# Attention stores its accumulators undivided; inverse sums travel through DRAM and the division moves to the mixing stage

## The reference

```python
qkv = x @ c_attn_w.T + c_attn_b                 # 16 heads of 16
q_lat, k_lat, v_lat = q @ q2l_w.T + q2l_b, k @ kv2l_w.T + kv2l_b, v @ kv2l_w.T + kv2l_b   # latents of 32
q_lat, k_lat = rope(q_lat), rope(k_lat)
att = einsum('bhql,bhkl->bhqk', q_lat @ wqk_w.T + wqk_b, k_lat) * 32 ** -0.5
att = softmax(where(causal, att, -inf))
y = (einsum('bhqk,bhkl->bhql', att, v_lat) @ l2o_w.T + l2o_b).transpose(0, 2, 1, 3).reshape(B, T, C)
x = layernorm(x + y @ cproj_w.T + cproj_b)
logits = relu(x @ rw1 + rb1) @ rw2 + rb2        # router over 8 experts, the best 2 of each token
x = layernorm(x + weighted sum of the two experts' outputs, 1024 places per expert)
```

## Time and profile before

| | us |
|---|---|
| timed runs, median of 3 | 2879.03 |
| profiled execution: span, first to last instruction | 2899.6 |
| TensorE matmul busy in it | 2746.4 (95%) |
| VectorE busy | 2128.1 (73%) |
| ScalarE busy | 1811.4 (62%) |
| GpSimd busy | 802.8 (28%) |

### The profile page before, as it was taken

How to read it: one execution, slowest core, us unless ns; L and a number is a source line. 1 busy time by engine, 2 the same in 40 slices (tenths; PEclk the granted TensorE clock), 3 DMA queues, 4 the chain that set the end, 5 groups by cost and what they waited for, 6 DMA issues and landing times. The chain is left out here.

```text
span 2899.6 us, 47875 instructions
## 1 busy us (share of the span) xinstructions
PE 2746.4 (95%) x16538; PEld 1913.0 (66%) x16538; DVE 2128.1 (73%) x5590; ACT 1811.4 (62%) x3353; POOL 802.8 (28%) x785
## 2 busy tenths in 40 slices
PE   8999989999999999999999999999799995999991
PEld 7888755666666666666566666665377773999991
DVE  7888889988898888888888888887144543545444
ACT  5666626667667766777776677776554452555554
POOL 7888720110111111111011111101125444133322
PEclk9999979999999999999999999999899997999996
DMA  7788853432522424343252343330333211334326
GB/s 227 271 276 282 283 134 72 96 84 56 123 72 73 109 73 98 81 117 78 56 123 59 73 93 83 76 78 7 103 127 107 95 65 47 92 84 108 73 25 239
DMA packets 259522, 320.28 MB, mean 110 GB/s; under 512 B 70562, under 2 KB 157643, under 8 KB 258000
## 3 DMA queue, kind: packets, MB, share of 16 engines
q1 hardware_dynamic: 241616, 294.02, 36.0%
q0 software_dynamic: 17664, 23.19, 4.0%
HBM read 182.69 MB, written 143.95 MB: 113 GB/s over the span
## 5 line engine op out<-in xcount | busy, mean ns | idle before, releaser
L1027 ACT ACTIVATE att_probs<-att_score_bank 128x512 f32<-128x512 f32 (+1 forms) x2240 | 1131.7, 594 | 462.7 <-PE att_score_bank L954 449.6
L1082 DVE TENSOR_REDUCE att_partial_max<-att_max_bank 128x1 f32<-128x512 f32 x1536 | 983.1, 684 | 163.1 <-PE att_max_bank L940 162.5
L954 PE MATMUL att_score_bank<-att_q_st,att_k_st 98*128 98x512 f32 (+3 forms) x1792 | 574.4, 382 | 6.4 <-DMA att_q_st<-att_max_rows 4.6
L940 PE MATMUL att_max_bank<-att_k_st,att_q_st 96*128 96x512 f32 (+3 forms) x1792 | 566.3, 372 | 0.8 <-DVE att_partial_max L1086 0.2
L1067 POOL TENSOR_SCALAR_AFFINE_SELECT att_probs<-att_probs 128x512 f32<-128x512 f32 x256 | 162.6, 637 | 1406.0 <-ACT att_probs L1027 1406.0
L971 PE MATMUL att_acc_bank<-att_probs,att_v_st 128*32 128x512 f32 (+3 forms) x5120 | 528.5, 535 | 0.2
L1086 DVE CUSTOM_DVE_ANT_0 att_edge_sum<-att_max_bank,first_edge 128x256 f32<-128x256 f32 (+3 forms) x1024 | 460.8, 485 | 57.6 <-PE att_max_bank L940 56.9
L954 PEld LDWEIGHTS att_score_bank<-att_q_st,att_k_st 98*128 98x128 f32 x1792 | 319.1, 190 | 172.5 <-ACT att_probs L1027 83.2
L940 PEld LDWEIGHTS att_max_bank<-att_k_st,att_q_st 96*128 96x128 f32 x1792 | 330.7, 190 | 122.9 <-DVE att_partial_max L1082 49.9
L971 PEld LDWEIGHTS att_acc_bank<-att_probs,att_v_st 128*32 128x32 f32 x5120 | 136.5, 109 | 245.9 <-issue 133.5
L242 POOL TENSOR_TENSOR proj_op_low<-proj_turned,proj_op_high 128x512 fp32r<-128x512 f32 x192 | 244.6, 1300 | 47.1 <-ACT proj_op_high L402 45.1
(11 more groups left out here) (239 smaller groups left out, 4451.8 us busy)
## 6 DMA issues: line engine op xcount, KB each, us to landing
qk_parts<-proj_parts SPq DMA_DIRECT2D x64, 1024.0 KB, 5.2
att_k_st<-qk_parts SPq DMA_DIRECT2D x168, 256.0 KB, 6.1
att_q_st<-qk_parts SPq DMA_DIRECT2D x159, 256.0 KB, 4.2
v_tokens<-proj_v_tok SPq DMA_DIRECT2D x64, 256.0 KB, 4.6
att_v_st<-v_tokens SPq DMA_DIRECT2D x64, 256.0 KB, 6.8
exp_w<-in_ew SPq DMA_DIRECT2D x16, 1024.0 KB, 8.1
first_q<-qk_parts SPq DMA_DIRECT2D x33, 256.0 KB, 4.2
dispatched<-att_empty_rows SPq DMA_DIRECT2D x8, 1036.0 KB, 4.1
```

Of the source, the lines that this page charges most:

```text
L940: last = nc.tensor.matmul(max_ps[u % MAXB][:, at:end], q_tile(n)[0:3 * L, head, tile * P:(tile + 1) * P], k_tile(g, kb)[0:3 * L, head, 0:e ...
L954: last = nc.tensor.matmul(score_ps[h % SCOREB][:, i * (CH - q0):(i + 1) * (CH - q0)], k_tile(g, kt // TT)[:, j + i, (kt % TT) * P:(kt % TT ...
L1027: nc.scalar.activation(probs[:, k % PROBS, j:j + heads, q0:CH], score_ps[h % SCOREB][:, 0:heads * (CH - q0)].rearrange("p (j n) -> p j n", ...
L1082: nc.vector.tensor_reduce(partial_max[:, m % 2, j * TT + t, kb:kb + 1], bank[:], AX.X, ALU.max).then_inc(unit_reduced, 1)
```

## The change

In attention, `turn_sums`, `divide` and `bias_y` go, with their tiles and semaphores, and with the turns in `Order`. ScalarE's copy of the accumulator is stored as it is, 32 rows per head by 512 queries, undivided. SP loads the sums alone in the form of 128 x 64 for 512 tokens, VectorE inverts these, SP stores the inverses to DRAM, waits for that, and loads them with each head's row repeated on 16 partitions. The values come in already turned; `scale_y` on VectorE multiplies them with the spread inverses into `yt`. `turn_y` and `copy_y` go. The inverses of the first two chunks and the spread of the first are made in the last two slots of attention. The bias of the values is folded into `kept.b_out`, group by group. In `experts` two semaphores become one.

```diff
+def load_values(sp, d, chunk, yk, done):
+    for k in range(KC):
+        sp.dma_start(yk[:, k],
+                     heads_of(d)[chunk, k * P // HD:(k + 1) * P // HD, 0:HD]).then_inc(done, 16)
+def load_sums(sp, d, chunk, sums, done):
+    sp.dma_start(sums,
+                 heads_of(d)[chunk, :, HD].rearrange("h (i n) -> h i n", n=PARTS_OF_SUMS)).then_inc(done, 16)
+def store_recips(sp, d, chunk, recips, done):
+    sp.dma_start(d["recip"][chunk].rearrange("h (i n) -> (h i) n", n=PARTS_OF_SUMS), recips).then_inc(done, 16)
+def load_recips(sp, d, chunk, rk, done):
+    for k in range(KC):
+        src = d["recip"][chunk, k * P // HD:(k + 1) * P // HD]
+        sp.dma_start(rk[:, k],
+                     src.unsqueeze(1).broadcast_to([P // HD, HD, CH])).then_inc(done, 16)
...
-            nc.vector.tensor_scalar(bias_col[:], ones[:], lat[0][0][0:64, 64:65], l2o_b[:], ALU.mult, ALU.add).then_inc(weights_done, 1)
+            for g in range(G):
+                last = nc.vector.tensor_scalar(bias_col[:, g], ones[:], lat[0][0][0:64, 64 + g:65 + g], l2o_b[:],
+                                               ALU.mult, ALU.add)
+            last.then_inc(weights_done, 1)
...
             def store_y(n):
-                sp.wait_ge(y_biased, n + 1)
-                sp.dma_start(d["y"][b, c, :, :, col:col + HG * HD],
-                             y[:, n % 2].rearrange("p t j e -> p t (j e)")).then_inc(y_out[n % 2], 16)
+                sp.wait_ge(acc_read, n + 1)
+                sp.dma_start(d["y"][g // G, c, g % G], y_raw[:, n % 2]).then_inc(y_out[n % 2], 16)
...
                 if kt == 0 and n:
-                    pe.wait_ge(y_done, n)
+                    pe.wait_ge(acc_read, n)
...
             def read_acc(n):
                 act.wait_ge(weighted, LAST_STEP[n])
                 if n >= 2:
-                    act.wait_ge(y_done, n - 1)
+                    act.wait_ge(y_out[n % 2], 16 * (n // 2))
...
+            def sums_of(chunk):
+                load_sums(sp, d, chunk, sums[:, chunk % SUBS], sums_in[chunk % SUBS])
+            def spread(chunk):
+                buf = chunk % SUBS
+                sp.wait_ge(recip_done, chunk + 1)
+                store_recips(sp, d, chunk, recips[:, buf], recips_out)
+                sp.wait_ge(recips_out, 16 * (chunk + 1))
+                sp.wait_ge(y_scaled, KC * (chunk - SUBS + 1))
+                load_recips(sp, d, chunk, rk[buf], recip_in[buf])
...
             def step(c):        # SP
-                    load(chunk[3], (c[1] + 3) % SUBS)
+                    load(chunk[3])
+                if not is_last(c, 2):
+                    spread(c[1] + 2)
+                if not is_last(c, 4):
+                    sums_of(c[1] + 4)
...
             def step(c):        # TensorE
-                if not is_last(c, 2):
-                    turn_y(after(c, 2))
                 second_layer(c)
...
+            def scale_y(c):
+                buf = c[1] % SUBS
+                ready(dve, chunk_in[buf], count(c, 48, 48, bufs=SUBS))
+                ready(dve, recip_in[buf], count(c, 16 * KC, 16 * KC, bufs=SUBS))
+                ready(dve, mixed, count(c, 2))
+                for k in range(KC):
+                    nc.vector.tensor_tensor(yt[:, k], yk[buf][:, k], rk[buf][:, k], ALU.mult).then_inc(y_scaled, 1)
...
             def step(c):        # VectorE
                 split_x1(c)
+                if not is_last(c, 2):
+                    recips_of(after(c, 2))
                 if not is_first(c):
                     n = choose(after(c, -1))
                 if not is_last(c, 1):
                     moments_of(after(c, 1))
                 if not is_first(c):
                     place(after(c, -1), n)
+                if not is_last(c, 2):
+                    scale_y(after(c, 2))
```

More of the change, by code:

```diff
@@ L377, in _ @@
             for g in range(G):
-                last = nc.tensor.matmul(lat[1][0][:, 0:C], bias_col[:], cproj[:, g], start=(g == 0), stop=(g == G - 1))
+                last = nc.tensor.matmul(lat[1][0][:, 0:C], bias_col[:, g], cproj[:, g], start=(g == 0), stop=(g == G - 1))
             last.then_inc(folded, 1)
@@ L600 @@
 class Plan:
-    __slots__ = ("now", "last", "tiled", "u", "h", "w", "t", "vector", "scalar", "pool", "reduced", "exped", "ready",
-                 "weighed", "rows", "read", "divided", "before", "kind", "due")
+    __slots__ = ("now", "last", "tiled", "u", "h", "w", "vector", "scalar", "pool", "reduced", "exped", "ready",
+                 "weighed", "rows", "read", "before", "kind", "due")
     def copy(self):
         p = Plan()
[L608 to L611, removed]
+        (p.now, p.last, p.tiled, p.u, p.h, p.w, p.vector, p.scalar, p.pool, p.reduced, p.exped, p.ready, p.weighed,
+         p.rows, p.read) = (
+            self.now, self.last, self.tiled, self.u, self.h, self.w, self.vector, self.scalar, self.pool,
+            self.reduced, self.exped, self.ready, self.weighed, self.rows, self.read)
         p.before = self
@@ L687, in weigh @@
         if KS[k][2] == 0 and n:
-            if plan.divided[0] < n - 1:
-                return None
-            free = max(free, plan.divided[1])
+            free = max(free, plan.read)
         start = max(plan.now + INTO_TILES * (not plan.tiled),
@@ L698, in weigh @@
             p.read = p.scalar + 0.05
[L699 to L706, removed]
         return p
@@ L724, in search @@
         p.now = p.last = p.vector = p.scalar = p.pool = 0.0
-        p.tiled, p.u, p.h, p.w, p.t = False, 0, 0, 0, 0
+        p.tiled, p.u, p.h, p.w = False, 0, 0, 0
         p.reduced, p.exped, p.weighed = (0.0,) * MAXB, (0.0,) * SCOREB, (0.0,) * PROBS
-        p.ready, p.rows, p.read, p.divided = (), (), None, (-1, 0.0)
+        p.ready, p.rows, p.read = (), (), 0.0
         p.before = p.kind = None
         plans = [p]
-        for _ in range(NU + NS + NK + CHUNKS):
+        for _ in range(NU + NS + NK):
             alike = {}
@@ L1129, in _ @@
                     combine_max(UNITS_THROUGH.index(u + 1))
[L1130 to L1134 removed]
+                if u + 1 == UNITS_THROUGH[chunk_of(SLOTS - 1, 0)]:
+                    first_recips()
 EPS = 1e-5
@@ L1465, in norm @@
                                          scale=rstd[:, sub, t:t + 1]).then_inc(x1_done, 1)
-            def copy_y(c):
-                for k in range(KC):
-                    ready(act, y_turned, count(c, KC, k + 1))
-                    if not is_first(c):
-                        ready(act, mixed, count(c, 2))
-                    nc.scalar.activation(yt[:, k], xt_ps[k][:], ACT.Copy).then_inc(turned_copied, 1)
             def step(c):
@@ L1510, in split_x1, with recips_of @@
                                             ALU.subtract).then_inc(x1t_split, 1)
+            def scale_y(c):
[3 more added lines that the diff above has]
+                ready(dve, mixed, count(c, 2))
+                for k in range(KC):
+                    nc.vector.tensor_tensor(yt[:, k], yk[buf][:, k], rk[buf][:, k], ALU.mult).then_inc(y_scaled, 1)
+            def recips_of(c):
+                buf = c[1] % SUBS
+                ready(dve, sums_in[buf], count(c, 16, 16, bufs=SUBS))
+                nc.vector.reciprocal(recips[:, buf], sums[:, buf]).then_inc(recip_done, 1)
             def moments_of(c):
```

210 lines of the change are left out of this document (86 added, 124 removed).

## The result

The changed kernel takes 2891.7 us (median of 4 runs, 2890.2 to 2896.7), the kernel before 2881.1 beside it: a ratio of 1.0043, 95% interval 1.0031 to 1.0055. The two medians differ by 10.6 us; 2842 was forecast.

What follows compares the result with a forecast made beforehand. It took TensorE to bound attention and mixing, with VectorE close behind in attention. Terms 28.2 + 6 + 1.8 + 0.4 + 0.7 = 37 us off the median 2879.03 gave 2842 us, range 2816 to 2862.

Steps and rivals of the forecast that it cites:

- the slack of the round trip in mixing: Mixing steps: reciprocals go to DRAM and return spread, scaled values ready 5.4 us before TensorE wants them; cost 0.
- Rival 3: Mixing: the reciprocals' round trip is late in every step, 2.9 us each, 41 lost; 2883 us, chance 0.05.
- the same 37 off the median: Whole kernel: the 37 us gain reckoned on the profiled span of 2899.6 was taken off the timed median, 2879.03.
- VectorE's term (6): Attention: of 43.2 us of VectorE work removed, TensorE feels 6 us, bounds 8 lost to 15 gained.
- TensorE's 28.2: Attention: four transposes per chunk go, 0.44 us for each of 64 chunks, gained in full, 28.2 us.
- Rival 2: Attention: the planner's new order wastes part of the gain, leaving 17 to 20 us; 2861 us, chance 0.13.
- Rival 1: Attention: VectorE sets the pace, so its 43.2 us are gained, 46 in all; 2833 us, chance 0.16.
- The transposes of mixing: Mixing steps: TensorE's 8 transposes per step cover a wait for ScalarE, so removing them gives only 0.7 us.
- Multiplies and reciprocal hidden: Mixing steps: VectorE's added multiplies (1.4 us) and reciprocal (0.3 us) fall in its idle time; cost 0.
- Edge of the stages and start: From attention's last copy into mixing: 1.8 us gained at the edge, 0.4 us at mixing's start.
- Projection and experts 0: Projection's three more column fills and experts' two semaphores made one: 0 us.
- Wider loads at half the rate: Mixing: by the skill's rule, 256 KB loads use 8 engines, half the rate; values then ready about 2262.4, still ahead of TensorE.

Runs made afterwards that it cites:

- e1: The kernel before, unchanged, profiled once more in a single run: span 2879.5 us.
- e8: The kernel before without VectorE's reciprocal and multiply and GpSimd's bias add per chunk in attention, TensorE's transposes kept: 7.9 us faster.
- e7: The kernel before without TensorE's four transposes of each chunk's accumulator in attention, their places left empty in the order: 6.5 us faster.
- e12: The kernel before, its order unchanged, without attention's transposes, reciprocal, multiply and bias add, accumulator free with ScalarE's copy: 12 us faster.
- e13: Kernel of e9 with the planner of the kernel before, each turn's place left empty: 14.6 us slower than e9.
- e4: The changed kernel with TensorE's four transposes per chunk put back in attention, 63 of 64, unread: 31 us more.
- e9: Changed kernel, mixing steps with reciprocals made a step earlier and their store and spread both issued ahead of SyncE's loads: 2858 us.
- e11: The changed kernel without store and spread of the reciprocals in the mixing steps; what stays of sums, reciprocals and multiplies costs 1 us at most.
- e14: The changed kernel with one edit, reciprocals' store and spread ahead of the loads in SyncE's mixing step: 2856.9 us, ratio 0.9915 to the kernel before.
- e5: Changed kernel, mixing steps with the reciprocals' store ahead of SyncE's loads and reciprocals made a step earlier: no better than with the store moved alone.
- e6: The kernel before with an unused 128x64 VectorE reciprocal added ahead of the choice of experts in 14 mixing steps: 2.3 us less.

## Why the prediction was wrong

- **The step that failed: the slack of the round trip in mixing.** The prediction gave it 5.4 us and a cost of 0. In the late step shown above it was overdrawn by 2.9. Four terms were off, and they add up. The queue was seen rightly, the store behind the loads, but it leaves 9.96 us after the step's mixing begins, not 8.3 (1.6 lost; three loads take 1.8 us to issue, not 1.2, and start later). Behind 1 MB of loads it takes 5.76 us (5.7 to 6.5 in 12 of the 14 steps), not the 2.2 of a store on an idle queue (3.6 lost). The spread takes 5.57 us up to the multiplies, not 3.9 (1.7 lost; 5.0 to 5.7 in the steps in time, 5.6 to 6.4 in the late ones, where the 512 KB store of the normalized rows is issued 1.9 to 2.3 us behind it). And TensorE comes back after 19.7 us, not 21.23 (1.5 lost). 5.4 - 8.4 = -3.0, the 2.9 seen. Even with steps of 21.23 the values would have been 1.5 us late.
- **Rival 3 named the mechanism**, with a chance of 0.05. Its price of 2.9 us per step is close to the measured 2.7 (37.5 / 14) by luck: it had the worst landing of both transfers in every step, where in fact seven of 14 steps waited 2.7 to 4.0 us and paid some 1.7 more for the clock.
- **The base was one execution 20 us above the timed runs**, and the prediction took that offset as evenly spread ("the same 37 off the median"). Most of it sat in mixing, in the step length on which the slack rests. The rows had a sign of it: TensorE busy for 309.5 us of 335 in a stage said to be led by it. In that execution TensorE waited 13.6 us, in 14 waits, for ScalarE's hidden activations, of which e1 has none, and an instruction of the choice of experts stood beside GpSimd's add, 1.8 to 3.1 us long, in 8 of 14 steps, in e1 in none. Which of these is the cause, and what began it, is open.
- **A late value costs more than the wait.** The prediction counted only the wait; behind each of the seven waits the matmuls ran at a granted clock of 0.67 or so, some 1.7 us more.
- **Attention: right in direction, 24.3 us instead of 34** (19 to 24 by the other profiles with the same attention). VectorE's term (6) came out as sized, 5.2 in attention and 7.9 in the time (e8), though only in the old order. TensorE's 28.2 was the term that was mis-sized. It took 99% busy for "no idle time to hide it", while the weight loads' waits of 104.7 and 81.8 us stood in the earlier trace rows. In the order written with turns only 6 of it come out (e7), and those waits grow by 27.9. Both parts together give 8.6 (e12), and the order written anew 15.8 (e13). Rival 2 had the right place, the new order, and the wrong sign; that its number for attention, 20, is near the measured one is luck. Rival 1 fell in the old order: with all of VectorE's 43 us gone attention is 5.2 shorter (e8). In the new order no run puts VectorE's work back, but 63 turns of TensorE cost 30 us there in full (e4), which speaks against VectorE setting the pace. That a turn without cover costs 0.48 us shows that the price itself was read well from the earlier trace rows.
- **The transposes of mixing were free**: right. Steps are 19.7 us with them (e1) and without (e9), and the 0.78 us wait has taken their place.
- **Multiplies and reciprocal hidden**: right (e11). **Edge of the stages and start**: 2.2 predicted, 1.5 measured. **Projection and experts 0**: right, from the first mixing matmul of the last chunk to the end 502.8 us in e1 and in the changed kernel.
- **Wider loads at half the rate**, the rule of the Trainium skill (DMA: Bandwidth & Descriptors, the section on why a DMA increments its semaphore by 16) on the slowest dimension: the trace agrees. The last spread of the changed kernel has the queue to itself. Its 512 KB, in two loads with a slowest dimension of 8, move from 2371.82 to 2375.18 at 156 GB/s with the DMA engines busy for 0.50 of the time; the store of the normalized rows, also 512 KB, moves from 2385.6 in 1.67 us at 311 GB/s and 0.88. Those 1.7 us more are about as much as the spread's term was short. They don't decide the matter alone: ahead of the loads, the same spread costs nothing (e9, e14).

## What to carry to other kernels

Before a slack is reckoned from a profile, its execution's span has to be held against the timed runs; where it is off, find the stage that holds the difference, or count the slack with the shortest step that the engine's own work allows. A transfer's landing time has to be taken for its place in the queue: here the same 32 KB store landed in 1.5 us ahead of 1 MB of loads and in 5.7 to 6.5 behind them, so the short transfer that someone waits for goes ahead of the long ones that nobody does. What an operation costs in an order written by a planner is known only together with the order that is written without it.

## What was not expected of the hardware

VectorE's small instructions are held up beside a GpSimd add of two SBUF operands. In e5:

```profile
2188.13 0.19 DVE L1568 TENSOR_TENSOR mix_cand<-mix_rest,mix_top 128x32 f32<-128x32 f32 x1
2188.36 3.08 DVE L1569 TENSOR_TENSOR mix_cand<-mix_cand,mix_rev 128x32 f32<-128x32 f32 x1
2191.47 0.19 DVE L1570 TENSOR_REDUCE mix_rank<-mix_cand 128x4 f32<-128x32 f32 x1
```
```profile
2188.95 2.42 POOL L1347 TENSOR_TENSOR mix_xb<-kept_xr,kept_b_out 128x1024 f32<-128x1024 f32 x1
```

The multiply of 0.19 us takes 3.08 and ends with the add, at 2191.4. It starts 0.6 us before the add does, so either the add's recorded start is late or it holds VectorE earlier than the trace shows. The Trainium skill (SBUF — State Buffer, the section on the two separate sides) says that a VectorE operation with two SBUF inputs and a GpSimd operation that reads SBUF take a shared port pair in turn, each for its whole length, the first to start going first. The trace agrees in that VectorE stands for the add's 2.4 us and more; by the recorded starts VectorE was first here, and it was held up all the same. It cost nothing where it caught the last instruction of the choice (10 steps of e6, 3 of e14, all of 19.7 us). Whether it costs something in the middle of the choice, as in e5 and in the first profile, no run tells.
